# First and last token columns of a token-mixing step: made for four feature tiles together on VectorE, and put in place by ScalarE

## The reference, cut to what matters

```python
def _time_shift(x):
    return jnp.pad(x, ((0, 0), (1, 0), (0, 0)))[:, :-1, :]
...
h = _layer_norm(x, ln1_g, ln1_b)
hh = _time_shift(h)
k = (h * tm_mk + hh * (1 - tm_mk)) @ Wk.T
v = (h * tm_mv + hh * (1 - tm_mv)) @ Wv.T
r = (h * tm_mr + hh * (1 - tm_mr)) @ Wr.T
...
h = _layer_norm(x, ln2_g, ln2_b)
hh = _time_shift(h)
kk = (h * cm_mk + hh * (1 - cm_mk)) @ Wkey.T
sr = jax.nn.sigmoid((h * cm_mr + hh * (1 - cm_mr)) @ Wcr.T)
```

## Time and profile before

| | us |
|---|---|
| median of 3 runs | 1052.47 |
| lowest, highest | 1048.45, 1054.65 |
| profiled execution, its own time | 1050.13 |
| span of the profiled execution | 1048.3 |
| TensorE waits for the first load | 3.9 |
| TensorE waits for VectorE's L1754 and L1750, from 577 us on | 3.3 and 2.2 |
| TensorE waits for GpSimd's L2035 | 0.7 |
| TensorE waits for ScalarE's L1020 and L990 | 0.2 and 0.2 |

### The profile page before, as it was taken

One profiled execution on the slowest core, in us unless ns is written; L12 is line 12 of the kernel. 1 busy time (PEld: TensorE's weight loads), 2 busy tenths in 40 slices (PEclk: granted clock), 3 DMA queues, 4 the chain that ended last, 5 costly groups with the idle time before them and its releaser, 6 DMA issues.

```text
span 1048.3 us, 13496 instructions
## 1 busy us (share of the span) xinstructions
PE 1035.0 (99%) x4616; PEld 854.9 (82%) x4616; DVE 713.6 (68%) x1231; ACT 520.4 (50%) x874; POOL 618.3 (59%) x508
## 2 busy tenths in 40 slices
PE   8999999999999999999999999989999999999999
PEld 7887888888888888888888888778878888888887
DVE  7899866785545564566568667768689566666655
ACT  7867888765444454323345333433435334444442
POOL 7796574644765545445547665569664356565652
PEclk9999999999999999999999999999999999999999
DMA  9100325277653344745633766675736445445432
GB/s 352 53 21 0 62 80 121 87 249 269 214 195 112 131 161 142 232 148 128 169 86 119 245 218 241 145 257 201 216 146 220 151 155 179 157 154 161 160 102 81
DMA packets 81123, 165.60 MB, mean 158 GB/s; under 512 B 39072, under 2 KB 39456, under 8 KB 76192
## 3 DMA queue, kind: packets, MB, share of 16 engines
q1 hardware_dynamic: 65600, 116.43, 33.6%
q0 software_dynamic: 15168, 48.24, 15.4%
q10 hardware_dynamic: 288, 0.09, 0.0%
HBM read 101.80 MB, written 58.74 MB: 153 GB/s over the span
## 4 chain that ended last, share of the span: by engine, by line
PE 86%; DVE 4%; DMA 3%; SPq 3%; POOL 2%; issue 1%; ACT 1%; DVEq 0%; ACTq 0%
PE bank L651 13%; PE bank L652 13%; PE bank L653 13%; PE bank L662 13%; PE bank L663 13%; PE bank L664 13%; PE bank L823 2%; PE bank L822 2%; PE bank L824 2%; SPq L544 2%; DMA rows<-row_stats 2%; POOL operand L2035 2%; PE bank L726 1%; DMA quart<-wide 1%; DMA extra<-rows 0%
## 5 line engine op out<-in xcount | busy, mean ns | idle before, releaser
L662 PE MATMUL bank<-combo,left 128*128 128x512 f32 x672 | 262.4, 390 | 5.5 <-DVE bank L1754 3.3
L664 PE MATMUL bank<-combo,left 128*128 128x512 f32 x672 | 261.6, 389 | 0.0
L663 PE MATMUL bank<-combo,left 128*128 128x512 f32 x672 | 261.6, 389 | 0.0
L2108 POOL TENSOR_TENSOR inner<-made,inner 128x512 fp32r<-128x512 f32 x96 | 129.4, 1369 | 124.9 <-ACT inner L1146 124.9
L1661 DVE TENSOR_TENSOR resid<-bank,resid 128x512 f32<-128x512 f32 x176 | 119.8, 686 | 117.7 <-PE bank L653 116.8
L2068 POOL TENSOR_TENSOR left<-quart,left 128x512 fp32r<-128x512 f32 x96 | 116.3, 1234 | 83.1 <-ACT left L1113 40.6
L662 PEld LDWEIGHTS bank<-combo,left 128*128 128x128 f32 x672 | 126.2, 188 | 34.3 <-DVE bank L1754 4.8
L651 PE MATMUL bank<-right,inner 128*128 128x512 f32 x384 | 149.5, 389 | 0.0
L653 PE MATMUL bank<-right,inner 128*128 128x512 f32 x384 | 149.5, 389 | 0.0
L652 PE MATMUL bank<-right,inner 128*128 128x512 f32 x384 | 149.5, 389 | 0.0
L664 PEld LDWEIGHTS bank<-combo,left 128*128 128x128 f32 x672 | 126.2, 188 | 26.3
(11 more groups left out here) (199 smaller groups left out, 2001.7 us busy)
## 6 DMA issues: line engine op xcount, KB each, us to landing
kept_left<-left SPq DMA_DIRECT2D x24, 1792.0 KB, 8.1
left<-kept_left POOLq DMA_DIRECT2D x24, 1024.0 KB, 7.4
left<-kept_left POOLq DMA_DIRECT2D x24, 768.0 KB, 5.0
quart<-wide SPq DMA_DIRECT2D x24, 512.0 KB, 4.1
tall_staged<-tall SPq DMA_DIRECT2D x48, 256.0 KB, 5.2
raw<-kept SPq DMA_DIRECT2D x32, 256.0 KB, 6.4
landed<-wts SPq DMA_DIRECT2D x20, 256.0 KB, 5.3
resid<-x POOLq DMA_DIRECT2D x4, 1024.0 KB, 9.4
```

The lines of the kernel that those rows point to most:

```text
L662: pe.matmul(acc[:], hi, combo[:, c, k, 0, :], start=fresh and k == 0, stop=False, skip_group_check=True)
L663: pe.matmul(acc[:], hi, combo[:, c, k, 1, :], start=False, stop=False, skip_group_check=True)
L664: mm = pe.matmul(acc[:], lo, combo[:, c, k, 0, :], start=False, stop=k == 1, skip_group_check=True)
L2108: pool.tensor_tensor(inner[:, h % 4, i, 1, :], made_at(n), inner[:, h % 4, i, 0, :].bitcast(F32), ALU.subtract).then_inc(inner_lo, 1)
```

## The change

The edge and the first column of all four tiles are made together. `ends(norm, b)` on VectorE multiplies, in one instruction, column 0 of the four banks by whole_g and column 511 by rest_g, for all mixes of the norm (24 products per partition in time mixing, 16 in channel mixing). The result goes to `opening[b % 2]` and `edge[b % 2]`. A second instruction adds the edge of the block before to the opening, and a third (not in the last block) adds the bias to the edge. The four banks A become one PSUM tensor, `front`, so that one operand reaches over them.

For k and v of all blocks, for cr of block 1 and for ck of the other blocks, ScalarE copies the openings to column 0: two tiles at a time behind rest 1 and behind rest 3 (`opening_columns`, 18 copies of 128x2), and all four tiles of ck ahead of its rests (3 copies of 128x4). For r of all blocks, cr of blocks 0, 2 and 3 and ck of block 1 (`opens_norm`), VectorE still makes the first columns one by one.

`ends` stands right behind mix r(b) in time mixing. In channel mixing it stands behind mix cr of blocks 0, 2 and 3, and for block 1 behind mix ck, ahead of mix cr. `last_token` stood in other places: (0, 0) behind the first wkv_weight, (0, b) in the middle of the output's additions, (1, 1) ahead of mix ck. ScalarE's rests of the operands whose openings it copies wait for `ends_scaled`, which the product sets. The copies wait for `opening_made`, which the second instruction sets.

```diff
+            def opening_columns(kind, b, tiles):
+                n, m = operand_at(kind, b) + tiles.start, MIXES[kind]
+                act.wait_ge(opening_made, BLOCKS * (kind == "cr") + b + 1)
+                act.activation(made[:, n % RING:n % RING + KT // 2, 0], opening[b % 2][:, m, tiles],
+                               ACT.Copy).then_inc(rest_part, 1)
...
             def operand_hi(kind, b, k):
                 n = operand_at(kind, b) + k
                 act.wait_ge(op_made, n + 1)
+                if kind != "y" and not opens_norm(kind, b):
+                    act.wait_ge(rest_part, opened_by(kind, b, k))
...
             def rest_of(kind, b, k):
...
                 act.wait_ge(transposed, KT * b + k + 1)
+                if not opens_norm(kind, b):
+                    act.wait_ge(ends_scaled, BLOCKS * (kind == "cr") + b + 1)
...
             def rest_of_ck(b):
                 act.wait_ge(t2_psum, KT * (b + 1))
+                if not opens_norm("ck", b):
+                    act.wait_ge(ends_scaled, BLOCKS + b + 1)
+                    act.wait_ge(opening_made, BLOCKS + b + 1)
+                    act.activation(held[:, b, :, 0], opening[b % 2][:, MIXES["ck"], :], ACT.Copy).then_inc(ck_rest, 1)
...
+            def ends(norm, b):
+                transposed, ms, beta = ((t1_psum, slice(0, 3), 1), (t2_psum, slice(3, 5), 3))[norm]
+                n = ms.stop - ms.start
+                done = BLOCKS * norm + b
+                columns = front[:, :, 0:BT:BT - 1].rearrange("p (o k) t -> p t o k", o=1).broadcast_to((P, 2, n, KT))
...
+                dve.wait_ge(transposed, KT * (b + 1))
+                dve.tensor_tensor(both_ends[:, b % 2, :, ms, :], columns, gains[:, :, ms, :],
+                                  ALU.mult).then_inc(ends_scaled, 1)
+                dve.wait_ge(ends_scaled, done + 1)
+                if b:
+                    dve.wait_ge(last_taken, (BLOCKS - 1) * norm + b)
+                tile = opening[b % 2][:, ms, :]
+                dve.tensor_tensor(tile, tile, edge[(b + 1) % 2][:, ms, :], ALU.add).then_inc(opening_made, 1)
+                if b + 1 < BLOCKS:
+                    tile = edge[b % 2][:, ms, :]
+                    dve.tensor_tensor(tile, tile, vec[:, beta:beta + 1, :].broadcast_to((P, n, KT)),
+                                      ALU.add).then_inc(last_taken, 1)
...
             mix("r", 0)
+            ends(0, 0)
             matrix_lo(ITEM_K, range(2))
...
             mix("r", 1)
+            ends(0, 1)
...
                     norm2_moments(b - 1, s)
-                    if s == 1 and b + 1 < BLOCKS:
-                        last_token(0, b)
...
                     mix("r", b + 1)
+                    ends(0, b + 1)
...
             mix("cr", 0)
-            last_token(1, 0)
+            ends(1, 0)
             mix_ck(0)
             gated_value(BLOCKS - 1)
-            last_token(1, 1)
             mix_ck(1)
+            ends(1, 1)
             mix("cr", 1)
             mix("cr", 2)
-            last_token(1, 2)
+            ends(1, 2)
             mix_ck(2)
...
             mix("cr", 3)
+            ends(1, 3)
             mix_ck(3)
```

More of the change, by code:

```diff
@@ L68, in mixed_before, with opens_norm, rest_before, rest_by @@
     return len([piece for piece in ORDER[:ORDER.index((kind, b))] if piece[0] != "y"])
+def opens_norm(kind, b):
+    return kind == "r" or kind == ("ck" if b == 1 else "cr")
+def rest_before(kind, b):
+    return sum(KT if opens_norm(*piece) else KT + 2 for piece in ORDER[:ORDER.index((kind, b))] if piece[0] != "y")
+def rest_by(kind, b, k):
+    return rest_before(kind, b) + k + 1 + (0 if opens_norm(kind, b) else k // 2)
+def opened_by(kind, b, k):
+    return rest_before(kind, b) + 3 * (k // 2 + 1)
+def ck_rest_by(b, k):
+    return KT * b + k + 1 + len([c for c in range(b + 1) if not opens_norm("ck", c)])
 PAIRS = BLOCKS // 2
@@ L268, in build @@
         vec = sb("vec", [P, len(VECTORS), KT])
[L269 to L272, removed]
+        gains = sb("gains", [P, 2, len(MIXES), KT])
+        whole_g, rest_g = gains[:, 0], gains[:, 1]
+        both_ends = sb("both_ends", [P, 2, 2, len(MIXES), KT])
+        opening, edge = ([both_ends[:, n, end] for n in range(2)] for end in range(2))
+        whole_b = edge[1]
         back = sb("back", [P, BLOCKS, SUBS])
@@ L341, in build @@
         seventh = e2
-        bank = [ctx.enter_context(nc.psum_tensor(f"bank{i}", [P, 512], F32)) for i in range(8)]
-        A, B = bank[:4], bank[4:]
+        front = ctx.enter_context(nc.psum_tensor("front", [P, KT, 512], F32))
+        bank = [ctx.enter_context(nc.psum_tensor(f"bank{i}", [P, 512], F32)) for i in range(KT, 8)]
+        A, B = [front[:, k, :] for k in range(KT)], bank
         X, Y, V, Z = B
@@ L1079, in mixed @@
                     rest_of(kind, b, k)
+                    if k % 2 and not opens_norm(kind, b):
+                        opening_columns(kind, b, slice(k - 1, k + 1))
                     if k == behind:
@@ L1486, in norm1_scaled @@
                     dve.tensor_tensor(bank_of, tile, scale, ALU.mult).then_inc(t1_psum, 1)
[L1488 to L1497, removed]
@@ L1502, in mix, with first_column @@
+            def first_column(tile, b, m, k):
+                return dve.scalar_tensor_tensor(out=tile[:, 0:1], in0=A[k][:, 0:1], scalar=whole_g[:, m, k:k + 1],
+                                                in1=edge[(b + 1) % 2][:, m, k:k + 1], op0=ALU.mult, op1=ALU.add)
             def mix(kind, b):
                 n, m = operand_at(kind, b), MIXES[kind]
-                parts = KT * mixed_before(kind, b)
-                if b:
-                    dve.wait_ge(last_taken, KT * (b + (BLOCKS - 1 if kind == "cr" else 0)))
+                if b and opens_norm(kind, b):
+                    dve.wait_ge(last_taken, b + (BLOCKS - 1 if kind == "cr" else 0))
@@ L1507, in mix @@
                 for k in range(KT):
-                    dve.wait_ge(rest_part, parts + k + 1)
+                    dve.wait_ge(rest_part, rest_by(kind, b, k))
                     tile, share = made_at(n + k), whole_g[:, m, k:k + 1]
[L1510 to L1513, removed]
+                    mixed = dve.scalar_tensor_tensor(out=tile[:, 1:BT], in0=A[k][:, 1:BT], scalar=share,
+                                                     in1=tile[:, 1:BT], op0=ALU.mult, op1=ALU.add)
@@ L1527, in last_of_r_lo @@
+                    if opens_norm("ck", b):
+                        mixed = first_column(tile, b, m, k)
+                    mixed.then_inc(ck_made, 1)
             def last_of_r_lo():
@@ L1933, in _ @@
             wkv_weight(0, range(1))
-            last_token(0, 0)
             wkv_weight(0, range(1, 2))
```

24 lines of the change are left out of this document (14 added, 10 removed).

## The result

The changed kernel took 1058.44 us (median of 11 runs) against 1050.88 us for the kernel before, measured beside it. The ratio is 1.0073, with a 95% interval of 1.0063 to 1.0084: 7.6 us slower. One of the 11 runs, at a granted clock of 0.85, took 1155.66 us and is left out of the ratio. I had forecast 1053.9 us, in a range up to 1057.0, and "same" with a chance of 0.89. The forecast is wrong: the loss is more than five times the +1.4 us of my sum, and lies above its upper bound of +4.6 us. The profiled execution took 1056.93 us, with a span of 1055.1 us.

The account below looks back on a forecast made before the run. TensorE was taken to bound the kernel. Five terms, 0.5 + 0.2 - 0.4 + 0.8 + 0.3 = +1.4 us, on 1050.13 us profiled gave 1051.5; with 2.3 us up to the runs' median, 1053.9 us, range 1049.5 to 1057.

Parts of the forecast that it names:

- What bounds the kernel: TensorE, busy 1035.0 of 1048.3 us; VectorE's time counts only where TensorE waits, at most 0.9 us to gain.
- What comes: Instructions added on VectorE and ScalarE; each VectorE addition 0.17 us at best, 1.38 us at worst beside busy GpSimd.
- Rival (c): ends() itself is long, holding the queue 4 us at three places before operands: some 7 us, 1059.5 us; chance 0.07.
- Both signs of being wrong: No TensorE wait near 197 us, or TensorE's waits before 245 us growing by over 3 us in sum.
- The base: Median of the runs, 1052.47 us, 2.3 us over the profiled execution's 1050.13 us; that difference was added to the forecast.
- VectorE's busy time: 22.5 us removed, 4 to 21 us added; 8 to 14 us less expected, about 702 us busy.
- Term 1: First k operand, k0, delayed by ends(0, 0) ahead of K's low parts: +0.5 us, between 0 and 1.4.
- Term 2: r of block 1, delayed by opening copies in ScalarE's queue ahead of v0's third tile: +0.2 us, between 0 and 0.7.
- Term 3: Relief from block 1's edges taken earlier, against waits at 94.78 and 104.16 us: -0.4 us, between -0.42 and 0.
- Term 4: cr of block 1: ScalarE's rests start later, its sigmoids free output(3)'s bank late near 197 us: +0.8, between 0 and 1.2.
- Term 5: cr of block 2 and ck2: ScalarE's delay and a held addition make output(3, 0) late near 208 us: +0.3, between 0 and 1.3.

Follow-up runs that it names:

- e1: Kernel before, plus one unused 128x8 VectorE addition with both inputs in SBUF behind mix cr0: 1058.89 us in one execution.
- e5: Changed kernel, GpSimd's DMA issue of block 2 moved behind cr0's low parts, its wait for VectorE's norm kept in place: 1052.03 us, ratio 1.0009.
- e9: e5 and e8 joined, with ends(0, 2) and ends(0, 3) also moved behind the gated value of the block before: 1049.78 us, ratio 1.0001.
- e3: Changed kernel, GpSimd's DMA issue of block 2 moved behind cr0's low parts together with its wait for the norm: 1053.30 us, ratio 1.0023.
- e4: Changed kernel, GpSimd waiting for its own third low part of the cr weights before the fourth, DMA issue unmoved: 1049.99 us in one execution.
- e6: The kernel of e4 again, timed against the kernel before: 1051.97 us, ratio 1.0012.
- e2: Kernel before, plus the same unused VectorE addition as e1 but with its first input in PSUM: 1047.31 us in one execution.
- e10: Control: kernel before with only the DMA issue moved behind cr0's low parts and its wait kept: 1049.86 us, ratio 0.9998.
- e7: e6 with ends(0, 1) moved behind gated_value(0) on VectorE: 1052.77 us, ratio 1.0021 to the kernel before.
- e8: e7 with first columns of k0 and v0 made by VectorE again and ends(0, 0) moved behind the first wkv_weight: 1051.41 us, ratio 1.0004.

## Why the prediction was wrong, step by step

**What bounds the kernel** was right: VectorE's time counts only where TensorE waits, and no version gained over the kernel before.

**What comes, the addition's upper bound**, is the step that failed. "An addition is thus 0.17 us at best and 1.38 us at worst" was read from L1564, L1476 and from GpSimd's plain rows. Behind a DMA issue the worst is the whole row: 7.92 us in the changed kernel and 8.15 us in e1. The cue stood in the trace of the kernel before, which I had before me. GpSimd's four low parts of the cr weights there take 5.55 us and the single ones 1.8 us, where those of the earlier trace rows take 5.06 and 1.32 us, at the same distance of 1.25 us (GpSimd's timeline of the kernel before):

```profile
174.71 1.27 POOL L2029 DMA_DIRECT2D resid<-x  x1 [11.30 <-DVE held L1593]
175.48 5.55 POOL L2023 TENSOR_TENSOR weights<-landed,weights 128x512 fp32r<-128x512 f32 x4
180.51 5.50 POOL L2035 TENSOR_TENSOR weights<-made,weights 128x512 fp32r<-128x512 f32 x4
```

I had written that the durations of successive instructions overlap by up to 0.1 us. Here they overlap by 0.5. No VectorE instruction in that stretch had two SBUF inputs, so nothing showed what it does. The bound should have gone to the end of these eight, at 186.01, some 8 us behind the end of mix cr0 at 177.87.

**No term for ends(1, 0).** With that bound it needed one. I had summed five places and left this one out, and my text gives no reason. Additions held as I had pictured it would have cost nothing there: in e5 they took 0.34 and 1.33 us, and TensorE did not wait. With the long hold the place was worth 5.4 us of waiting and 1.5 us of the lower clock, of which my text had nothing. Rival (c) put the loss into each ends() at 3.5 us and came to 1059.5 us. The size is close by chance, the mechanism is another: seven of the eight opening additions took 0.2 to 1.2 us. Both signs of being wrong that I had named came: no wait near 197 (some 206 in the changed kernel), and the waits of TensorE before 245 us grew from 0.9 to 8.3 us (1.15, 0.32, 1.41 and 5.41).

**The base.** The 2.3 us that I added for the runs came from a median of three, 1052.47. With eleven runs it is 1050.88, 0.75 us over the profiled execution. Over the right base my sum would have given 1052.3 us, still further from the 1058.44 measured.

**VectorE's busy time.** I expected 702 us. 719.6 us were measured, of which the 14 additions are 18.4 (L1547 14.0 and L1550 4.4, by lines), and would be 2.2 at 0.16 us each. The one addition alone is 7.9. In e9 it is 711.9 us.

**The five terms** are seen in the runs without the long hold, as the difference of TensorE's stretches to the kernel before. Up to 174 us the changed kernel, e3, e4, e5 and e6 are the same code, and so are the kernel before, e1, e2 and e10, so that these executions show the scatter of a single one.

- Term 1, r0 to the transposes of block 1's first norm (28.54 us before): +0.3 us in e3 and e6, +1.2 to +1.4 in the changed kernel, e4 and e5. It goes with the third instruction of ends(0, 0), which took 0.16 us in the two and 1.33 or 1.34 in the three. I had 0.5, between 0 and 1.4.
- Term 2, from there to output(0) (18.44 before), where r of block 1 stands: +1.4 us in the changed kernel, +0.2 or +0.3 in the four others. I had 0.2, at most 0.7. The 1.4 is a wait for the gated value of block 0, which receptance(1) waits for and which I had not named.
- Term 3, output(0) to output(1): 43.52 us in the changed kernel, e4 and e5, 44.23 in e6, 45.45 in e3, against 44.42 and 44.38 in the kernel before and e2 and 45.74 and 45.76 in e1 and e10. The means, 44.0 and 45.1 us, speak for a relief, but no pair of executions shows its size. I had -0.4.
- Term 4, the transposes of block 1 to output(3): +0.6 us in e4 and e6 (15.15 in e6 for 14.54 us, with the wait for the sigmoid L1139 near 198 that I had named), and I had 0.8. In e5 it was nothing: 14.32 us, as in its control e10.
- Term 5: +0.3 us in e4 and e6, as forecast.

From r0 to the feed-forward part e6 took 1.2 us more than the kernel before, near the +1.4 us of the sum. Part of that is luck: e4, the same kernel, took 1.65 us more than the kernel before.

**That TensorE's clock stays up** I had assumed without a word. Waits of 5.41 us, of 5.82 (e1), of 1.83 (e3) and of 1.93 (e7, in the feed-forward part) came with a stretch at 1.2 GHz. Waits of 1.4 us at 25.97 (e4) and 51.95, of 1.63 at 106.50 (e9) and of 2.46 us (e6, in the feed-forward part) did not. So the length of a wait alone does not decide it.

## What to carry to other kernels

When VectorE instructions are fused into fewer ones, look at where the new ones read. The old columns had their first input in PSUM and never stood in GpSimd's way. The new additions have two inputs in SBUF, and beside a busy GpSimd they cost up to one of its instructions each, or, behind a DMA issue on GpSimd's queue, all of its row. An instruction with one SBUF tile is not always free of this: the norm (L1649) took 1.51 us for each of its last three tiles in e3, where four take 1.91 otherwise, and the copy L1476 took 1.33. Read the spacing against the duration of GpSimd's instructions: where they overlap, a VectorE instruction with two SBUF inputs got in only when the row ended, and a wait of GpSimd for its own result, or the DMA issue moved behind the row, ended the overlap. A moved issue takes the overlap along to what comes next on GpSimd. And before an edit is aimed at a wait that one profile shows, look for it in a second execution of the same code.

## What was not expected of the hardware

GpSimd's instructions behind its own DMA issue started 0.5 us before the ones ahead had ended, at an unchanged distance of 1.25 us, until GpSimd had once run dry or had waited for a result of its own (in the changed kernel from 177.68 to 188.08, in e4 up to the pause at 181.06, in e5 for the four low parts from 186.06). The profile's spans of GpSimd are rough, so the 0.5 us is a sign to be looked for and not a measure. A VectorE instruction with two SBUF inputs was kept out until the overlap ended: for 7.92 us, 8.15 (e1) and 1.83 (e4, and 1.82 to 1.85 in e6, e7 and e8, which have the same pause). Beside rows without the overlap the additions lasted 1.34 us at most, about one instruction of GpSimd.

The Trainium skill (SBUF — State Buffer, section "Summary: rules for kernel authors") has the second of the two block until the first finishes. The trace agrees where GpSimd's instructions don't overlap. Behind a DMA issue the measurement goes further: the addition waited for the end of eight instructions, five of which had started over 1.2 us after it. The Trainium skill (GPSIMD Engine Reference, section "Instruction dispatch") says that each of GpSimd's cores starts the next instruction once it is through with its own share, whatever the other cores still do. The overlapping rows fit that, but no run here shows the single cores. That it is the overlap which never leaves a gap is an inference from e3, e4 and e5. No run made the overlap in another way than by a DMA issue.
